# Layer 1 of a two-layer attention and expert kernel: the shared units of its feed-forward part moved behind the attention's drain, its experts' weights sent in another order and at other times

## The chip, the cores and the metric

The kernel runs on one core of one Trainium2 chip. A core has a matrix engine (TensorE, "PE", with its weight load "PEld"), a vector engine (VectorE, "DVE"), a scalar engine (ScalarE, "ACT"), a general engine (GpSimd, "POOL") that also issues the indexed DMAs, and a queue engine (SyncE, "SP") that issues the plain ones. They share an on-chip memory (SBUF), an accumulator memory (PSUM) of 8 banks, and 16 DMA engines to the main memory. The metric is the device time of one execution in microseconds; lower is better.

## The reference, cut to what matters

Eight sequences of 256 tokens, 256 wide, go through two layers, each an attention and a mixture of experts, each added to what came in. The part that is changed is the second mixture of experts:

```python
x = x + _L1_attn_ref(_layernorm(x), ...)
x = x + _L1_ffn_ref(_layernorm(x), ...)

def _moe_forward(...):                       # E = 32 experts, K = 8 chosen for each token
    scores = sigmoid(x @ router_w)           # 4 of 8 groups of experts, then the best 8
    routed = sum over the 8 chosen of gate * ((silu(x @ w_gate[e]) * (x @ w_up[e])) @ w_down[e])
    shared = (silu(x @ sw_gate) * (x @ sw_up)) @ sw_down      # for every token
    return routed + shared
```

All is computed in float32; the attention's projections are split in a high and a low part.

## The kernel before, in words

**Stages.** Attention 0, the mixture of experts 0, then one stage for layer 1: `attention(..., 1, ...)`, `finish`, `expert_blocks`. Within the stage each engine has one program, in the order in which these three functions emit it; engines meet by semaphores alone.

**Attention 1** is a software pipeline written out by hand. The outer loop runs over rounds `i` from -3 to B + 3 = 11 (B = 8 sequences), the inner over 8 steps `j`. In round `i` sequence `i` has its scores and maxima made, `i - 1` its exponentials and its product with the values, `i - 2` its output projection, and `i - 3` and `i - 4` the front of the mixture of experts. Rounds 9, 10 and 11 are the drain: no scores are left, only the last links of sequences 5 to 7.

**The front of one sequence m** is a chain over four engines: DVE adds the projection (`out_add`) and takes the statistics (`front_stats`), POOL makes the reciprocal deviation (`front_rstd`, step 1 of round m + 3), ACT applies it (`front_apply`), PE transposes (`front_transpose`, L698), ACT copies (`front_xT`, L904), PE makes the logits (`front_logits`, L707), ACT the exponential (`front_exp`, L911), DVE chooses (`route_groups` to `route_chosen`, L1136 to L1177), PE transposes the choice (`front_chosen`, L716), ACT copies (`front_chT`, L917), PE counts ranks (`front_ranks`, L726 to L733), DVE turns them into places (`route_places`, L1195 to L1206). That last instruction counts up `f_placed`.

**Scatters.** The token rows go to their experts' regions in main memory by 128 indexed DMAs of POOL (`scatter_rows`, L1553), 16 for each sequence, in order; those of sequence m wait for `f_placed` of m + 1. From round 4, step 3 on POOL issues two a step, so 74 are issued when round 8 ends, 90 after round 9; the last 6 are left to `finish`.

**Weights.** `wres` holds the 32 experts' weights of layer 1 (384 KB each) at the top of the SBUF. Experts 26 to 31 lie in free room and are loaded at the start of the stage. The others lie over attention 1's tiles. SP sends 25 down to 5 once all exponentials' inputs and maxima are done (`st_ps`, `max_done`), one for each count of the semaphore `paced`, which POOL counts up after every second scatter from number 78 on (`PACED`). Experts 0 to 4 go in one DMA in `finish`, once all sequences are placed.

**Shared units.** The shared expert is 8 units of 512 tokens and half the hidden width: `up` (PE, L1477, into banks 0 and 1 or 2 and 3), `silu` (ACT), `keep` (DVE, L1490), `down` (PE, L1496, into the same two banks), `add` (DVE, L1503). `up` of unit u waits for `add` of u - 2. Four units stand in the drain, at the steps that `unit_pe`, `unit_act` and `unit_dve` list (rounds 9 and 10), the other four in `finish`, between the links that make the table of blocks: `count` (L1850), `first` (L1855), `table` (L1860).

**Expert blocks.** 159 blocks of 128 rows, each loaded (`e_xg`, L1974), turned, multiplied and scattered back. SP loads the first rows when the table stands and all 128 scatters have landed. PE's first `up` (L1996) waits for all weights and for the eighth unit's `add`.

## Time and profile before

| | us |
|---|---|
| median of 3 runs | 1170.13 (1168.87 to 1175.76) |
| the profiled execution | 1172.08 |
| its span, from the first to the last instruction | 1169.5 |
| PE busy in the span | 899.2 (77%) |
| DVE, ACT, POOL busy | 685.6, 467.1, 621.2 |

The profile is one execution. Its page gives busy times, the chain of work that ended last, and the groups of instructions; the trace behind it answers for any stretch, engine or line. Times in its rows count from the start of the span. Mixture of experts 0 ends at about 475 us, attention 1 with its drain at about 800, `finish` at about 830, the expert blocks at about 1112; the rest sums up and stores.

### The profile page before, as it was taken

The page shows a single profiled execution, that of the slowest core. Times are in us where ns is not written, and L with a number is a line of the kernel's source. Part 1 is how long each engine was busy: PE and PEld are TensorE (multiplying, and loading weights), DVE is VectorE, ACT ScalarE, POOL GpSimd, SP SyncE. Part 2 cuts the span into 40 slices and gives each one's busy share as a digit, 9 for nine tenths or more (in the row PEclk, how much of TensorE's full clock was granted, in tenths as well). Part 3 has the DMA queues.
Part 4 walks back from the last instruction along what each step waited for, and adds up shares of the span by engine and source line. Part 5 has one row for each costly group of instructions (what it writes and reads, how often), then busy time and mean ns, then how long its engine had stood idle before and what let it go on. Part 6 is the DMA issues. An engine that isn't in the chain of part 4 may idle for free.

```text
span 1169.5 us, 22075 instructions
## 1 busy us (share of the span) xinstructions
PE 899.2 (77%) x5927; PEld 691.8 (59%) x5927; DVE 685.6 (59%) x2692; ACT 467.1 (40%) x1176; POOL 621.2 (53%) x870
## 2 busy tenths in 40 slices
PE   1687989878597992379987888856899999989900
PEld 1465667657355881256665565533688887778700
DVE  4678888865532554467687674352455544444568
ACT  2346666743112441257655443311344444444400
POOL 3646666523163652336558888755356655545500
PEclk9859999988798996559989576787999999999955
DMA  8500000000624543400002222566455655545287
GB/s 231 192 2 1 2 2 1 1 2 1 263 106 127 152 130 120 144 1 2 2 29 86 85 97 101 210 222 221 147 163 174 182 157 161 153 141 156 70 327 319
DMA packets 73093, 136.97 MB, mean 117 GB/s; under 512 B 13406, under 2 KB 51725, under 8 KB 70928
## 3 DMA queue, kind: packets, MB, share of 16 engines
q1 hardware_dynamic: 52144, 85.15, 22.8%
q0 software_dynamic: 17632, 46.73, 11.2%
q10 hardware_dynamic: 3200, 3.70, 0.9%
q8 instruction: 53, 0.87, 0.3%
q14 instruction: 64, 0.52, 0.2%
HBM read 79.15 MB, written 62.39 MB: 121 GB/s over the span
## 4 chain that ended last, share of the span: by engine, by line
PE 36%; DVE 9%; POOL 6%; issue 5%; ACT 2%; another core or an unknown queue 1%; DMA 1%; DVEq 0%; POOLq 0%; ACTq 0%; SPq 0%
PE s_psum L1996 12%; PE s_psum L2009 6%; PE s_psum L1988 3%; POOL rows L1553 3%; PE s_psum L1477 3%; PE s_psum L2004 2%; DVE a_masked L1074 2%; DVE f_rows L2096 2%; DVE f_xT L2096 2%; PE s_psum L549 1%; POOL a_probs L1414 1%; PE s_psum L1496 1%; PE s_psum L646 1%; PE s_psum L602 1%
## 5 line engine op out<-in xcount | busy, mean ns | idle before, releaser
L2106 POOL DMA_INDIRECT parts<-e_y,e_dest x206 | 202.7, 984 | 180.7 <-DVE e_y L2079 96.9
L1996 PE MATMUL s_psum<-wres,e_xT 128*128 x824 | 213.9, 382 | 1.8 <-ACT e_xT L2036 1.0
L1996 PEld LDWEIGHTS s_psum<-wres,e_xT 128*128 128x128 f32 x824 | 156.1, 191 | 26.1 <-issue 5.4
L1414 POOL TENSOR_SCALAR_AFFINE_SELECT a_probs<-a_probs 128x256 f32<-128x256 f32 x256 | 107.5, 444 | 117.6 <-ACT a_probs L870 116.8
L1553 POOL DMA_INDIRECT rows<-f_rows,f_place_at x128 | 125.2, 978 | 40.3 <-issue 31.7
L2009 PE MATMUL s_psum<-wres,e_hT 128*128 x412 | 125.3, 386 | 12.2 <-ACT e_hT L2046 11.6
L870 ACT ACTIVATE a_probs<-s_psum 128x768 f32<-128x768 f32 x128 | 104.6, 817 | 72.8 <-PE s_psum L629 68.2
L2041 ACT ACTIVATE e_act_out<-s_psum 128x128 f32<-128x128 f32 x206 | 57.1, 277 | 180.8 <-PE s_psum L1996 101.6
L2070 DVE TENSOR_TENSOR e_hid<-e_act_out,s_psum 128x128 f32<-128x128 f32 x206 | 59.0, 286 | 91.8 <-issue 42.6
L1074 DVE CUSTOM_DVE_ANT_0 a_masked<-s_psum,a_ahead 128x128 f32<-128x128 f32 (+1 forms) x256 | 76.1, 353 | 42.0 <-PE s_psum L605 39.1
L2079 DVE TENSOR_SCALAR e_y<-s_psum,e_xg 128x256 f32<-128x256 f32 x206 | 99.6, 484 | 0.7 <-issue 0.7
L2036 ACT ACTIVATE e_xT<-s_psum 128x256 f32<-128x256 f32 x206 | 79.0, 383 | 36.5 <-PE s_psum L1988 34.3
L1074 DVE CUSTOM_DVE_ANT_0 m_rows<-s_psum,a_ahead 128x128 f32<-128x128 f32 (+1 forms) x256 | 76.0, 352 | 23.4 <-PE s_psum L605 22.9
L2078 DVE COPY e_dest<-e_xg 128x1 int32 x206 | 31.7, 154 | 89.6 <-PE s_psum L2009 61.0
L1988 PE MATMUL s_psum<-ident,e_xg 128*128 128x128 f32 x412 | 79.5, 276 | 1.8 <-DMA e_xg<-rows 1.7
L1988 PEld LDWEIGHTS s_psum<-ident,e_xg 128*128 128x128 f32 x412 | 58.5, 142 | 23.7 <-issue 3.0
L2009 PEld LDWEIGHTS s_psum<-wres,e_hT 128*128 128x128 f32 x412 | 62.1, 191 | 16.4 <-issue 15.5
L549 PE MATMUL s_psum<-qkv_hi,a_yT_hi 128*128 128x512 f32 (+2 forms) x96 | 43.5, 453 | 29.5 <-DVE a_yT_lo L1003 20.9
L855 ACT ACTIVATE a_qT<-s_psum 128x512 fp32r<-128x512 f32 x64 | 38.3, 601 | 66.3 <-PE s_psum L582 66.3
L602 PE MATMUL s_psum<-a_kT,a_qT 64*128 64x128 f32 x256 | 46.4, 357 | 21.1 <-DVE a_neg_max L1074 19.5
L2004 PE MATMUL s_psum<-ident,e_hid 128*128 128x128 f32 x206 | 57.0, 277 | 3.5 <-issue 2.9
L2046 ACT ACTIVATE e_hT<-s_psum 128x128 f32<-128x128 f32 x206 | 56.8, 276 | 6.2 <-PE s_psum L2004 5.0
(297 smaller groups left out, 1993.4 us busy)
## 6 DMA issues: line engine op xcount, KB each, us to landing
e_xg<-rows SPq DMA_DIRECT2D x159, 160.0 KB
f_rows<-parts SPq DMA_DIRECT2D x8, 1024.0 KB, 7.2
f_xT<-parts SPq DMA_DIRECT2D x8, 1024.0 KB, 7.4
wres<-in_experts SPq DMA_DIRECT2D x21, 384.0 KB
e_xg<-rows SPq DMA_DIRECT2D x47, 144.0 KB
wres<-in_experts SPq DMA_DIRECT2D x4, 1536.0 KB
rows<-empty SPq DMA_DIRECT2D x1, 5120.0 KB, 24.1
e_yk<-parts SPq DMA_DIRECT2D x16, 256.0 KB, 2.9
```

Source lines behind the costliest of these rows:

```text
L870: nc.scalar.activation(probs[:, j % NPB], ring[:, 2:4, 0:TRI], ACT.Exp, scale=exp_scale).then_inc(exp_done, 1)
L1074: last = nc.vector.tensor_tensor_reduce(out=masked[:, j % 2, hh, cols], in0=ring[:, hh, cols], in1=ahead[:, cols], scale=-1.0, scalar=BIG, ...
L1414: last = nc.gpsimd.affine_select(out=diagonal[:, :, a], in_=diagonal[:, :, a], compare_op=ALU.is_ge, fill=0.0, base=0, pattern=[[0, 2], [1 ...
L1553: nc.gpsimd.indirect_dma_start(out=front["table"][:, :], out_offset=bass.IndirectOffsetOnAxis(ap=front["place_at"][:, t, k:k + 1], axis=0) ...
L1988: last = nc.tensor.transpose(ps_x[b % 2][:, c * P:(c + 1) * P], xg[b % NX][:, c * P:(c + 1) * P], ident[:])
L1996: last = nc.tensor.matmul(ps_u[b % 2][:, 0:2 * P], xT[b % 2][:, c * P:(c + 1) * P], wres[:, ds(e, 1), 2 * c * P:2 * (c + 1) * P].rearrange ...
L2004: nc.tensor.transpose(ps_h[b % 2][:, 0:P], hid[b % 2][:], ident[:]).then_inc(h_ps, 1)
L2009: nc.tensor.matmul(ps_y[b % 2][:, 0:H], hT[b % 2][:], wres[:, ds(e, 1), D:D + H].rearrange("p a n -> p (a n)"), start=True, stop=True).the ...
L2036: nc.scalar.activation(xT[b % 2][:], ps_x[b % 2][:, 0:H], ACT.Copy).then_inc(xT_done, 1)
L2070: nc.vector.tensor_tensor(hid[b % 2][:], act_out[b % 2][:], ps_u[b % 2][:, P:2 * P], ALU.mult).then_inc(hid_done, 1)
L2079: nc.vector.tensor_scalar(y[b % NY][:], ps_y[b % 2][:, 0:H], pair[:, ds(e, 1), 0], None, ALU.mult).then_inc(y_done, 1)
L2106: nc.gpsimd.indirect_dma_start(out=parts[:, :], out_offset=bass.IndirectOffsetOnAxis(ap=dest[b % NY][:], axis=0), in_=y[b % NY][:], in_off ...
```

## The change

Four edits, all in layer 1:

- The tables `unit_pe`, `unit_act` and `unit_dve` are gone. All 8 units are in `finish`, behind all of the attention on each engine. On PE `up` of 0 and 1 come ahead of `count`; `first` comes behind `up` 2, `table` behind `up` 3.
- Weights: all of 25 down to 0 are single DMAs of SP in attention 1, each for one count of `paced`. 25 to 19 wait for the last transposes of the stacked tile (`group_ps`), 18 to 16, 15 to 13 and 12 to 5 for the shifted scores of ever later sequences, 4 to 0 for the last places. For this the tiles are allocated in another order.
- `paced` is counted up once a step in the 13 steps from round 7, step 0, and from round 9 on after every fourth scatter.
- Scatters: two a step up to round 9, one a step in rounds 10 and 11. So 106 are issued in the attention and 22 in `finish`.

```diff
-FREE_EXPERTS, LAST_EXPERTS = 26, 5
-PACED = 78
+STACK_EXPERTS, FIRST_QUERY_EXPERTS, SECOND_QUERY_EXPERTS = 19, 16, 13
+ROUND_STEPS = 13
+PACE = 4
...
-    unit_pe, unit_act, unit_dve = {}, {}, {}
-    if front is not None:
-        unit_pe = {(B + 1, 0): [("up", 0)], (B + 1, 2): [("up", 1)], (B + 1, 3): [("down", 0)], (B + 1, 5): [("down", 1)],
-                   (B + 1, 7): [("up", 2)], (B + 2, 1): [("up", 3)], (B + 2, 2): [("down", 2)], (B + 2, 6): [("down", 3)]}
...
-                sp.wait_ge(st_ps, PAIRS * B)
-                sp.wait_ge(max_done, PAIRS * B)
-                for n, e in enumerate(range(FREE_EXPERTS - 1, LAST_EXPERTS - 1, -1)):
+                sp.wait_ge(group_ps, NF * B)
+                for n, e in enumerate(range(FREE_EXPERTS - 1, -1, -1)):
+                    if e == STACK_EXPERTS - 1:
+                        sp.wait_ge(st_ps, PAIRS * (B - 2))
+                    if e == FIRST_QUERY_EXPERTS - 1:
+                        sp.wait_ge(st_ps, PAIRS * (B - 1))
+                    if e == SECOND_QUERY_EXPERTS - 1:
+                        sp.wait_ge(st_ps, PAIRS * B)
+                        sp.wait_ge(max_done, PAIRS * B)
+                    if e == LAST_EXPERTS - 1:
+                        sp.wait_ge(f_placed, B)
                     sp.wait_ge(front["paced"], n + 1)
                     sp.dma_start(env["wres"][:, e], front["w_experts"][e]).then_inc(front["wres_loaded"], 16)
...
                     if front is not None and (i, j) >= (4, 3):
-                        for _ in range(2):
+                        for _ in range(2 if i <= B + 1 else 1):
                             m = scattered // (TB * TOPK[layer])
                             if scattered % (TB * TOPK[layer]) == 0:
                                 pool.wait_ge(f_placed, m + 1)
                             scatter_rows(nc, front, layer, scattered)
-                            if scattered >= PACED and scattered % 2:
+                            scattered += 1
+                            if i > B and scattered % PACE == 0:
                                 passed(pool, front["paced"])
-                            scattered += 1
+                        if (B - 1, 0) <= (i, j) < (B - 1 + ROUND_STEPS // PAIRS, ROUND_STEPS % PAIRS):
+                            passed(pool, front["paced"])
...
-                if n % 2:
+                if n % PACE == PACE - 1:
                     passed(pool, front["paced"])
...
+            units["up"](pe, 0)
+            units["up"](pe, 1)
             count()
-            units["up"](pe, begun)
-            first()
-            units["up"](pe, begun + 1)
-            for u in range(begun, NU):
+            for u in range(end):
                 units["down"](pe, u)
-                if u == begun:
+                if u + 2 < end:
+                    units["up"](pe, u + 2)
+                if u == 0:
+                    first()
+                if u == 1:
                     table()
-                if u + 2 < NU:
-                    units["up"](pe, u + 2)
```

## Rows read from the trace of the kernel before

**Rows 1.** Stretches of attention 1 and drain: us, then each engine's busy us, PEclk, DMA share, GB/s
```profile
700.00:731.00 31.00, 26.85 (x181) 18.66 (x181) 13.83 (x66) 11.08 (x18) 26.23 (x42) 0.68 0.28 102
...
740.00:750.00 10.00, 8.54 (x51) 5.47 (x50) 4.23 (x12) 2.77 (x5) 7.62 (x10) 1.00 0.76 243
...
780.00:790.00 10.00, 0.39 (x2) 0.15 (x2) 4.79 (x27) 0.00 (x0) 7.56 (x9) 0.65 0.89 357
790.00:800.00 10.00, 1.57 (x6) 1.42 (x6) 0.66 (x5) 1.66 (x2) 4.77 (x5) 0.50 0.27 98
```

**Rows 2.** Units in rounds 9 and 10: busy us of L1477, then of L1496
```profile
731.00:761.00 30.00, 9.25 (x16) 3.71 (x16) 0.76 0.59 208
...
731.00:761.00 30.00, 5.65 (x16) 4.01 (x16) 0.76 0.59 208
```

**Rows 3.** Timeline of POOL: start, us, what, idle before and its releaser
```profile
758.54 0.96 POOL L1553 DMA_INDIRECT rows<-f_rows,f_place_at  x1 [0.30 <-issue]
759.80 0.96 POOL L1553 DMA_INDIRECT rows<-f_rows,f_place_at  x1 [0.30 <-issue]
769.11 0.23 POOL L1348 TENSOR_SCALAR a_f_var_eps<-a_f_mv 128x2 f32<-128x2 f32 x1 [8.35 <-DVE a_f_mv L1131]
...
770.47 0.22 POOL L1354 TENSOR_TENSOR a_f_shift<-a_f_neg_mean,a_f_rstd 128x2 f32<-128x2 f32 x1
...
821.79 0.96 POOL L1553 DMA_INDIRECT rows<-f_rows,f_place_at  x1 [0.30 <-issue]
```

**Rows 4.** Timelines of the front of sequence 7, and of one link of sequence 6
```profile
752.90 1.92 PE L707 MATMUL s_psum<-router,f_xT 128*128 128x32 f32 x8 [4.26 <-issue]
...
758.63 0.22 ACT L911 ACTIVATE a_f_exp<-s_psum 128x64 f32<-128x64 f32 x1 [4.48 <-DMA e_yk<-parts]
...
770.73 1.09 ACT L898 ACTIVATE f_rows<-x,a_f_shift,a_f_rstd 128x256 f32<-128x256 f32 x2 [2.87 <-POOL a_f_shift L1354]
...
775.75 0.60 PE L698 MATMUL s_psum<-ident,f_rows 128*128 128x128 f32 x4
...
776.38 0.60 ACT L904 ACTIVATE f_xT<-s_psum 128x512 f32<-128x512 f32 x1 [3.63 <-issue]
...
777.03 1.08 PE L707 MATMUL s_psum<-router,f_xT 128*128 128x32 f32 x8 [0.69 <-issue]
...
778.55 0.24 DVE L1136 TENSOR_SCALAR a_scores<-a_f_exp 128x64 f32<-128x64 f32 x1 [1.38 <-issue]
...
784.41 0.22 DVE L1177 TENSOR_TENSOR a_chosen_r<-a_replaced,a_eligible 128x64 fp32r<-128x64 f32 x1 [1.54 <-remote]
...
784.69 0.39 PE L716 MATMUL s_psum<-ident_r,a_chosen_r 128*32 128x128 f32 x2 [4.78 <-issue]
...
790.80 0.37 ACT L917 ACTIVATE a_chT<-s_psum 32x256 fp32r<-32x256 f32 x1 [12.29 <-remote]
...
791.23 0.42 PE L726 MATMUL s_psum<-a_base_r,ones_r 128*128 128x64 f32 x1 [6.14 <-issue]
...
792.19 0.60 PE L733 MATMUL s_psum<-tri_r,a_chT 32*128 32x32 f32 x2
...
799.30 0.19 DVE L1195 TENSOR_TENSOR f_cum<-f_cum,a_chosen_both 128x32 fp32r<-128x32 f32 x1 [9.86 <-remote]
```

**Rows 5.** Timelines of `finish` and of the first block
```profile
800.42 5.16 PE L1477 MATMUL s_psum<-f_xT,f_ws 128*128 128x512 f32 x8
...
811.01 0.80 PE L1860 MATMUL s_psum<-d_lists,d_ones 32*128 32x318 f32 x2
...
826.48 3.02 PE L1496 MATMUL s_psum<-f_ws,u_hid 128*128 128x256 f32 x8 [1.91 <-DVE u_hid L1490]
...
831.40 1.12 PE L1996 MATMUL s_psum<-wres,e_xT 128*128 x4 [1.05 <-ACT e_xT L2036]
...
811.12 1.23 DVE L1503 TENSOR_TENSOR x<-s_psum,x 128x1024 f32<-128x1024 f32 x1 [2.70 <-issue]
...
817.86 1.22 DVE L1503 TENSOR_TENSOR x<-s_psum,x 128x1024 f32<-128x1024 f32 x1 [4.54 <-PE s_psum L1496]
```

**Rows 6.** Timeline of SP's queue
```profile
770.48 10.73 SPq L1322 DMA_DIRECT2D wres<-in_experts  x10
...
825.41 24.47 SPq L1974 DMA_DIRECT2D e_xg<-rows  x20
```

More of the change, by code:

```diff
@@ L391, in attention, with query_homes @@
             place_top = sb("place_top", [P, TB, 8])
+        pieces = NH // 2 + (NK // 2 if multi else 1)
+        def query_homes(i):
+            return (sb(f"qT{i}", [P, PAIRS, N], F32R), sb(f"kT{i}", [P, PAIRS if multi else 1, N], F32R))
+        ahead = sb("ahead", [P, TRI])
+        masked = wide("masked", [P, 2, 2, TRI])
+        max_stack = sb("max_stack", [P, TB, 2, 2 * NH, 2], F32R)
+        maxT = sb("maxT", [P, TRI], F32R)
+        pairs_by_age = {i: query_homes(i) for i in (1, 0, 2)}
+        qT, kT = ([pairs_by_age[i][n] for i in range(NQ)] for n in range(2))
         yT_hi = sb("yT_hi", [P, FC, N], F32R)
@@ L402, in attention @@
         rotated = wide("rotated", [P, TB, QK])
-        pieces = NH // 2 + (NK // 2 if multi else 1)
         stack = sb("stack", [P, TB, pieces * P], F32R)
-        qT = [sb(f"qT{i}", [P, PAIRS, N], F32R) for i in range(NQ)]
-        kT = [sb(f"kT{i}", [P, PAIRS if multi else 1, N], F32R) for i in range(NQ)]
-        ahead = sb("ahead", [P, TRI])
-        masked = wide("masked", [P, 2, 2, TRI])
-        max_stack = sb("max_stack", [P, TB, 2, 2 * NH, 2], F32R)
-        maxT = sb("maxT", [P, TRI], F32R)
         m_E = EXPERTS[0]
@@ L808, in _ @@
                             moe_logits(int(name[1]))
-                    for name, u in unit_pe.get((i, j), []):
-                        if u == 0 and name == "up":
-                            pe.wait_ge(shared_loaded, 16)
-                            pe.wait_ge(exp_done, PAIRS * B)
-                            pe.wait_ge(max_done, PAIRS * B)
-                        front["units"][name](pe, u)
         @block.scalar
@@ L977, in _ @@
                         ln_apply(i + 3)
-                    if (i, j) in unit_act:
-                        front["units"]["silu"](act, unit_act[i, j])
         @block.vector
@@ L1299, in _ @@
                         moe_apply(m)
-                    for name, u in unit_dve.get((i, j), []):
-                        front["units"][name](dve, u)
             dve.wait_ge(out_added, B)
@@ L1798, in finish @@
     make_sem, psum, block = shared_stage
-    placed, wres_loaded, units, begun = front["placed"], front["wres_loaded"], front["units"], front["units_begun"]
+    placed, units, end = front["placed"], front["units"], NU
     with ExitStack() as ctx:
@@ L1861, in table @@
                                  skip_group_check=True).then_inc(tab_ps, 1)
+            pe.wait_ge(front["shared_loaded"], 16)
+            pe.wait_ge(front["exp_done"], PAIRS * B)
+            pe.wait_ge(front["max_done"], PAIRS * B)
+            units["up"](pe, 0)
+            units["up"](pe, 1)
             count()
[L1864 to L1867 removed]
+            for u in range(end):
                 units["down"](pe, u)
[L1869 removed]
+                if u + 2 < end:
[3 more added lines that the diff above has]
+                if u == 1:
                     table()
[L1871 to L1872 removed]
         @block.scalar
         def _(act):
[L1876 removed]
+            for u in range(end):
                 units["silu"](act, u)
@@ L1887, in _ @@
             dve.wait_ge(ones_made, 1)
+            units["keep"](dve, 0)
             dve.wait_ge(count_ps, 1)
@@ L1892, in _ @@
             nc.vector.tensor_copy(blocks[:], blocks_i[:]).then_inc(blocks_done, 1)
-            units["keep"](dve, begun)
+            units["add"](dve, 0)
+            units["keep"](dve, 1)
             dve.wait_ge(blocks_done, 1)
@@ L1903, in _ @@
             nc.vector.tensor_tensor(lists[:, NB:2 * NB], owned[:], start[:], ALU.mult).then_inc(lists_done, 1)
-            units["add"](dve, begun)
+            units["add"](dve, 1)
+            units["keep"](dve, 2)
             dve.wait_ge(tab_ps, 1)
             nc.vector.tensor_copy(tab[0:1, 0:2 * NB], ps_r[0:1, 0:2 * NB]).then_inc(tab_done, 1)
-            for u in range(begun + 1, NU):
+            units["add"](dve, 2)
+            for u in range(3, end):
                 units["keep"](dve, u)
```

15 lines of the change are left out of this document (3 added, 12 removed).

## The prediction

> **What bounds the kernel now.** I read the views in this order: the page's slices and its chain of waits, the busy times by stretch, then the timelines of each engine between the end of round 8 (about 734 us) and the first expert block.
>
> The change touches nothing outside layer 1's attention, drain and `finish`. In rounds 7 and 8 POOL is busy 26.23 of 31 us; what is left are its short gaps between instructions, and the chain of waits of that stretch runs over POOL's scatters and cuts [rows 1]. So the dense rounds are paced by POOL, and the DMA engines are used at 28% there. In the drain no engine is full. The front of a sequence is a chain of single instructions over four engines, and PE has four units woven in: 9.25 + 5.65 = 14.9 us of them before 761 us [rows 2], all in PE's order ahead of links that the chain waits for. In `finish` PE sets the pace: a unit every 817.86 - 811.12 = 6.74 us, and the first block's product starts at 831.40, right behind the eighth unit [rows 5]. The weights and the rows are not what ends last there: SP sends the first row loads at 825.41 [rows 6], four microseconds before PE is free.
>
> What stands out is time in which nobody works. From 785 to 799 us PE is nearly idle at the lower clock (granted 0.5 in 790:800, that is 1.2 GHz) [rows 1], and the consumers start late behind work that has ended: ACT's exponential of sequence 6 at 758.63, where the logits ended at 752.90 + 1.92 = 754.82, 3.8 us late; ACT's copy at 790.80, where PE's transposes ended at 784.69 + 0.39 = 785.08, 5.7 us late; DVE's first place at 799.30, where the ranks ended at 792.19 + 0.60 = 792.79, 6.5 us late; DVE's choice itself 1.5 us late [rows 4]. The profile names "remote" or nothing as releaser. I call these late handovers. They fall in stretches in which POOL issues scatters without pause and, just before, SP's weights fill the DMA engines (76 and 89% [rows 1]). The sum below depends on whether they stay.
>
> **The change, part by part.**
>
> *Dense rounds.* 13 weight loads of 384 KB are added, one in each of 13 steps; scatters per step stay two. POOL's additional instruction is a semaphore count, which before cost nothing visible: the gap in front of a scatter is the same 0.30 us at 758.54 and 821.79 whether a count stood there or not [rows 3]. The DMA engines have room: 28% used, and a load a step is less dense than 740:750, where they ran at 76% while POOL's scatters kept their 7.62 us of 10 [rows 1]. I take 0; its bounds are 0 and 3 us, by the thought that two or three handovers in these 13 steps come late by one more microsecond.
>
> *Drain, sequence 6 and the first part of 7.* The 14.9 us of units leave PE's order here. The statistics of sequence 7, which came at 769.11 and left POOL idle for 8.35 us [rows 3], come earlier by about that and by the 3.8 us handover if it is mended: near 752. But POOL then isn't ready. Its scatters of round 9 run on, one every 1.26 us, and the one at 758.54 (the single one of round 10, step 0) ends at 759.50 [rows 3]. So `front_rstd` of sequence 7 starts at 759.8 in place of 769.11: a gain of 9.3 us, not 17. It also means that lateness of up to 7 us ahead of this point costs nothing. It takes 770.47 + 0.22 - 769.11 = 1.6 us, to 761.4.
>
> *Drain, the rest of 7.* From rows 4: apply 1.09, transposes 0.60 at the full clock (I take 1.1, as the logits took 1.08 and 1.92 at the two levels), copy 0.60, logits 1.92, from there to DVE's first instruction 778.55 - 778.11 = 0.44, choice 784.41 + 0.22 - 778.55 - 1.54 = 4.54, transposes 0.39, copy 0.37, ranks 792.79 - 791.23 = 1.56. Sum 12.0, with half a microsecond for the handovers between them 12.5. The ranks end at 761.4 + 12.5 = 773.9, the places a microsecond later. Before, the ranks ended at 792.79.
>
> For PE's pieces I take the prices at 1.2 GHz, since with the units gone nothing fills PE in the drain, and in 790:800, where it did only such pieces, the granted clock was 0.50 [rows 1]. At 2.4 GHz the sum is 2.0 us less (0.5 + 0.84 + about 0.7), and the first unit would start warm, 5.16 - 3.7 = 1.5 less; that is the lower bound, -3.5. The Trainium skill (TensorE: Matmul & The Clock Gate, "What's actually happening") says that an idle PE is clocked at half rate; by it alone the slow prices hold, and the trace agrees with its 0.50. It speaks against moving work out of the drain.
>
> *Finish.* PE now starts unit 0 right behind the ranks, without waiting for the places, at 773.9. Four units took from 800.42 to 826.48 + 3.02 = 829.50, 29.1 us, slow start and slow last `down` included [rows 5]. Four more at 6.74 us are 27.0. `table` stood in the pause ahead of `up`, and now stands behind it: 0.8 us [rows 5]. DVE's list of blocks stands ahead of `add` 1 and delays `up` 3 by about 0.6. Together 57.5: the last `down` ends at 831.4 in place of 829.50, 1.9 us later.
>
> *Behind it.* POOL: from 761.4 on 37 scatters (91 to 127) at 1.26 us end at about 808, against 821.79 + 0.96 before [rows 3]; even with waits for landings they stay ahead of 829. Weights: the last follows scatter 123, at about 803, and is there by 810. Both are hidden behind the units by some 20 us; if that cover were gone they would count. SP's new waits for weights stand ahead of the row loads only, which need the table and all scatters anyway. POOL's sequencer counts `paced` when it reads past the scatters, not when they run: SP sent ten loads in 770.48 to 781.21, while the twenty scatters that pace them took twice as long [rows 6]. So "every fourth scatter" will be bursts of about four, not a stream. The Trainium skill (Advanced Engine Details and Errata, "Sequencer Loop") says that a sequencer reads and queues further instructions while earlier ones execute; the trace agrees, with these ten loads in 10.73 us.
>
> *The late handovers.* On the chain of sequence 7 they cost 1.5 + 5.7 + 6.5 = 13.7 us before. If the weights' traffic is the cause they mostly go, since bursts are now four loads and not ten. If POOL's unbroken scatters or PE's idleness are the cause they stay, because both remain, and PE idles more. So they cost between 0 and 13.7; I take 5. For the shorter bursts speaks that links at 767 to 769 us, with no traffic, were prompt; for the other that the last one at 799.30 came when the DMA share was 27% [rows 1].
>
> Sum: +1.9 + 5 = +6.9 us. The profiled execution took 1172.08, 2.6 more than its span 1169.5, and stands 1.95 over the median of 1170.13. I carry the difference to the median: 1177.0.
>
> **The rivals.**
>
> 1. *Handovers stay half late* (the forecast): +3 to +11 us, 1173 to 1181. Chance 0.41.
> 2. *Handovers become prompt.* Only the weights made them late. +1.9, and down to -1.6 at the full clock: 1168.5 to 1172.5. For it: late ones cluster behind bursts of 7 and 10 loads. Against it: bursts of four remain, and 799.30. Chance 0.27.
> 3. *Slower: the handovers stay as late as before.* The place is the front of sequence 7, from 761 to 775 us, price the whole 13.7: +15.6, 1185.7. It decides from 9.8 us of lateness on, where +1.9 + 9.8 reaches 1%. For it: POOL scatters without pause through all of it, and lateness before was worst with PE idle. Chance 0.24.
> 4. *Weights slow the dense rounds.* If each of 13 steps waits 1.2 us longer for something the loads hold up, 15.6 us, 1187 to 1193. Against it: 740:750, where POOL kept its pace. Chance 0.05.
> 5. *Faster by over 1%.* It needs 11.7 us. The drain can end no earlier than POOL lets it, and 8 units behind it take at least 54; that gives -1.6. Only if the lateness also sits in something that I don't see, such as the last scatters' landing, is there more. Chance 0.03.
>
> **How the numbers follow.** The forecast is rival 1's middle, 1177.0. Its own range is 1173 to 1181. The range that should hold 8 in 10 takes in rival 2's and most of rival 3: 1167 to 1189. One per cent (11.7 us) is about what a measurement of this kernel can tell from no change. Faster by over 1%: 0.03. Slower: rivals 3 and 4, 0.29, of which 0.01 stays under the bound, 0.28. Within 1%: 0.69.
>
> **What would show it.** Right: in the drain no `u_` tile; POOL's L1348 of sequence 7 at about 759.8 with no idle time before it; L716 to L733 of sequence 7 done near 774 plus the lateness; then 8 periods of 6.74 us on PE without a break up to 831 plus the lateness; the first e_xg load long before the last `down`; the expert blocks as before. The number that decides is the time from POOL's L1354 to PE's last L733, 12.5 us if handovers are prompt, up to 26 if not. Wrong: rounds 7 and 8 longer than 31 us for the same steps, POOL's sequence-7 statistics waiting for DVE again, or PE waiting in front of its first L1996 for weights.

## The result, and the profile after

The changed kernel took 1182.8 us (median of five runs, 1176.3 to 1192.4) beside 1169.4 us (1166.3 to 1175.8) for the kernel before: the ratio is 1.0147, with a 95% interval of 1.0098 to 1.0197. So it is slower, by 13.5 us. The forecast of 1177.0 is 5.8 us too low, and the time lies inside the range of 1167 to 1189. Throughout, an execution over 1.5% above the fastest of its kernel in the same session is left out of medians and ratios; that touched two of the kernel before and one of run 4. The profiled execution is the slowest of the five, 1192.38 us with a span of 1189.9, 20.4 us over the span of before; so the split below is that of a slow execution, and no trace splits the 13.5 us of the medians. These are the lines of it that answer to those of before, in the order of the chain. First POOL's and ACT's timelines (start, us, what, idle time before it and its releaser).

```profile
766.00 0.23 POOL L1343 TENSOR_SCALAR a_f_var_eps<-a_f_mv 128x2 f32<-128x2 f32 x1
...
767.30 0.20 POOL L1349 TENSOR_TENSOR a_f_shift<-a_f_neg_mean,a_f_rstd 128x2 f32<-128x2 f32 x1
```

```profile
774.70 0.22 ACT L901 ACTIVATE a_f_exp<-s_psum 128x64 f32<-128x64 f32 x1 [4.28 <-issue]
...
797.88 0.60 ACT L1481 ACTIVATE u_act_out<-s_psum 128x512 f32<-128x512 f32 x1 [11.90 <-DMA rope_gamma<-in_k_gamma]
```

DVE's timeline: the last instruction of the choice, three of the places, and the first `keep`.

```profile
782.45 0.23 DVE L1165 TENSOR_TENSOR a_chosen_r<-a_replaced,a_eligible 128x64 fp32r<-128x64 f32 x1 [3.09 <-remote]
...
788.83 0.19 DVE L1183 TENSOR_TENSOR f_cum<-f_cum,a_chosen_both 128x32 fp32r<-128x32 f32 x1 [1.82 <-remote]
...
792.95 0.29 DVE L1192 MAX8 a_place_top<-a_place 128x8 f32<-128x32 f32 x2 [3.66 <-remote]
795.06 0.17 DVE L1194 CAST f_place_at<-a_place_top 128x16 int32<-128x16 f32 x1 [1.82 <-remote]
...
799.43 0.69 DVE L1487 TENSOR_TENSOR u_hid<-s_psum,u_act_out 128x512 f32<-128x512 f32 x1 [3.94 <-DMA setup_tri<-in_tri]
```

PE's timeline from the logits of sequence 7 to the first block (L1474 is `up`, L1493 `down`), and SP's queue.

```profile
770.48 1.91 PE L703 MATMUL s_psum<-router,f_xT 128*128 128x32 f32 x8 [0.69 <-ACT f_xT L894]
783.87 0.40 PE L712 MATMUL s_psum<-ident_r,a_chosen_r 128*32 128x128 f32 x2 [11.48 <-DVE a_chosen_r L1165]
...
785.70 0.60 PE L729 MATMUL s_psum<-tri_r,a_chT 32*128 32x32 f32 x2
786.24 9.36 PE L1474 MATMUL s_psum<-f_xT,f_ws 128*128 128x512 f32 x16
...
800.18 3.03 PE L1493 MATMUL s_psum<-f_ws,u_hid 128*128 128x256 f32 x8 [3.51 <-DVE u_hid L1487]
804.53 5.31 PE L1474 MATMUL s_psum<-f_xT,f_ws 128*128 128x512 f32 x8 [1.32 <-DVE x L1500]
...
850.74 2.42 PE L1493 MATMUL s_psum<-f_ws,u_hid 128*128 128x256 f32 x8 [1.92 <-DVE u_hid L1487]
...
855.06 2.07 PE L1994 MATMUL s_psum<-wres,e_xT 128*128 x4 [1.05 <-ACT e_xT L2034]
```

```profile
685.84 125.53 SPq L1316 DMA_DIRECT2D wres<-in_experts  x26
822.53 46.62 SPq L1972 DMA_DIRECT2D e_xg<-rows  x16
```

The reader is to see four things. POOL comes to the reciprocal deviation of sequence 7 without idle time, at 766.00 (before 769.11, after 8.35 us of waiting [rows 3]). Between the links there is still time in which nobody works: ACT's exponential starts at 774.70 though the logits ended at 770.48 + 1.91 = 772.39, and DVE's own successive instructions, which need nothing but each other, come 3.09, 3.66 and 1.82 us apart. The first `down` stands at 800.18, 4.6 us behind the end of both `up`, because its `keep` on DVE waits behind those late places and behind ACT's late `silu`. And the rows and weights are no part of it: SP sends the first row loads at 822.53, 30 us before PE is free for them.

The trace behind these rows also holds the times at which semaphores counted, though not of every count. It shows where a late handover is lost: not between the count and the consumer, but between the producer's end and the count (us).

| kernel | producer, its end | its count | consumer, its start |
|---|---|---|---|
| before | PE, logits of 6: 754.81 | 758.61 | ACT, exponential: 758.63 |
| before | PE, ranks of 7: 792.80 | 799.21 | DVE, first place: 799.30 |
| changed | DVE, replaced values: 779.37 | 782.43 | DVE, choice: 782.45 |
| changed | DVE, product for the places: 789.29 | 792.93 | DVE, maxima: 792.95 |
| run 2 | PE, logits of 7: 772.50 | 785.43 | ACT, exponential: 785.45 |
| run 5 | PE, `down`: 800.08 | 819.11 | DVE, `add`: 819.13 |
| run 7 | PE, `down`: 815.59 | 848.45 | DVE, `add`: 848.47 |

The consumer stands ready and starts 0.02 to 0.09 us behind the count, so its instructions were not late. (Runs 2, 5 and 7 are experiments below.)

This is how the 20.4 us between the two profiled executions divide, split at the last pair of cuts of round 8 (733.27 and 739.66), the last rank and the first block's product:

| stretch | before | after | difference | forecast |
|---|---|---|---|---|
| up to the last cuts | 733.3 | 739.7 | +6.4 | 0 |
| to the end of the last rank | 59.5 | 46.6 | -12.9 | -18.9, or -13.9 with 5 us of lateness |
| to the first block's product | 38.6 | 68.8 | +30.2 | +20.8 |
| to the end | 338.1 | 334.8 | -3.3 | 0 |

### The profile page after: what moved, and what is told of

Read it like the earlier page. It is cut to its first block, busy times and chain, and to the rows that moved or that the text cites. A ratio compares the mean times of both kernels' runs of the same rounds, so it can differ in the third digit from the quotient of the medians.

```text
span 1189.9 us, 22097 instructions
## 1 busy us (share of the span) xinstructions
PE 919.0 (77%) x5927; PEld 707.2 (59%) x5927; DVE 688.3 (58%) x2692; ACT 461.7 (39%) x1172; POOL 621.5 (52%) x870
## 4 chain that ended last, share of the span: by engine, by line
PE 37%; DVE 9%; POOL 6%; issue 5%; ACT 2%; another core or an unknown queue 2%; DMA 1%; DVEq 0%; POOLq 0%; ACTq 0%; SPq 0%
PE s_psum L1994 11%; PE s_psum L2007 6%; POOL rows L1550 3%; PE s_psum L1986 3%; PE s_psum L1474 2%; PE s_psum L545 2%; DVE f_rows L2094 2%; DVE f_xT L2094 2%; PE s_psum L2002 1%; DVE a_masked L1062 1%; PE s_psum L1493 1%; POOL a_probs L1409 1%; PE s_psum L598 1%; PE s_psum L642 1%
## 5 line engine op out<-in xcount | busy, mean ns | idle before, releaser
L2034 ACT ACTIVATE e_xT<-s_psum 128x256 f32<-128x256 f32 x206 | 79.2, 384 | 32.0 <-PE s_psum L1986 27.3
L625 PE MATMUL s_psum<-a_maxT,sel_head 64*128 64x384 f32 x256 | 58.2, 452 | 0.0
```

The costliest lines, as they stand in the source:

```text
L2034: nc.scalar.activation(xT[b % 2][:], ps_x[b % 2][:, 0:H], ACT.Copy).then_inc(xT_done, 1)
```

## The experiments

The runs were made in four sessions on three chips, the last two sessions on the same chip: runs 1 to 4, then 5 to 7 and the changed kernel again, then 8 and 9, then 10 and 11. The medians of the kernel before in them were 1172.2, 1171.5, 1163.8 and 1135.4 us, so each time is compared only with the kernel before of its own session. (Part of that is the stretch behind the first block: 338.1 us in the first profile of before, 319.4 and 319.7 in runs 10 and 11.) What is compared across sessions are distances within a trace: from the shift of sequence 7 to its last rank, and from there to the end of the last `down` (all in us). The start of the first block counts from the start of the span. Lateness is what a chain or a unit takes over its prompt length. Each row is one profiled execution; the ratio is from all executions. Run 7 was executed once, and its additional scatters make its total meaningless.

| kernel | shift of 7 to last rank | last rank to last `down` | first block | ratio to before |
|---|---|---|---|---|
| before | 22.1 | 36.7 (4 units) | 831.4 | 1 |
| changed | 18.8 | 66.9 | 855.1 | 1.0147 |
| changed, once more | 24.0 | 64.6 | 860.6 | 1.0273 (1.0184 to 1.0361) |
| 1 weights alone | 17.9 | 50.1 (4 units) | 838.6 | 1.0103 (1.0053 to 1.0153) |
| 2 units alone | 32.1 | 58.4 | 856.9 | 1.0262 (1.0172 to 1.0353) |
| 3 no weights in the drain | 23.3 | 58.2 | 846.2 | 1.0129 (1.0034 to 1.0224) |
| 4 none in rounds 10 and 11 | 19.0 | 72.9 | 867.2 | 1.0244 (1.0140 to 1.0348) |
| 5 scatters held | 12.2 | 86.9 | 870.5 | 1.0301 (1.0214 to 1.0387) |
| 6 held early | 12.2 | 87.3 | 862.3 | 1.0251 (1.0171 to 1.0331) |
| 7 short rows | 25.0 | 104.3 | 892.5 | - |
| 8 small instruction between | 21.6 | 66.8 | 850.8 | 1.0190 (1.0137 to 1.0244) |
| 9 rest behind each fourth | 12.2 | 56.6 | 855.7 | 1.0160 (1.0111 to 1.0210) |
| 10 early, rest behind each eighth | 12.2 | 58.2 | 831.8 | 1.0143 (1.0100 to 1.0185) |
| 11 before, four rests | 11.3 | 30.9 (4 units) | 819.2 | 1.0105 (1.0070 to 1.0139) |

### First question: which part of the change costs, the weights or the units?

**1. Weights alone.** The changed kernel with the unit tables of before and `finish` of before.

```diff
+    unit_pe, unit_act, unit_dve = {}, {}, {}      # and the tables and loops of the kernel before
...
-            units["up"](pe, 0)
-            units["up"](pe, 1)
             count()
+            units["up"](pe, begun)
+            first()
```

> The changed kernel with its units back at their old places in the drain (rounds 9 and 10, four of them) and the old order of the second half; the weights and the scatters stay as changed. Theory W (13 loads in rounds 7 and 8 slow the dense rounds by 6 to 9 us, as the trace of the changed kernel shows 36.4 + 30.5 us for two rounds that took 32.1 + 25.8): 1176 to 1179, and the two rounds stay over 65 us. Theory U (the 13.5 us come from the units' new place alone, and the longer rounds are the clock of one execution): 1168 to 1172, and the two rounds are back at 58 to 60 us. Half of each, my own guess: about +7.

**2. Units alone.** The kernel before, with the tables taken out and `finish` of the changed kernel (the same diff the other way).

> The kernel before with one thing changed: all eight units stand behind the drain, in the changed kernel's order; weights (21 in one chain from the end of round 8 on, 5 at the end) and scatters as before. Theory W: the units cost about 6 us (1174 to 1177), and rounds 7 and 8 take 58 us as before. Theory U: 1180 to 1184. Rival: the long chain of single loads in the drain makes the handovers of sequence 7 as late as before (13.7 us), then 1184.

Run 1 came out 1.0% slower and run 2 2.6% slower. The changed kernel, which has both, had been 1.5% slower in the first comparison and was 2.7% slower when it was run again. With such a spread the ratios can't tell how the parts add up; the traces have to. Theory W was wrong about the cost of the loads. In run 1 a stretch of 31 us in the two rounds with the loads moved twice the bytes of before (208 GB/s in place of 97) with POOL as busy (26.22 us in both):

```profile
682.00:713.00 31.00, 27.51 (x227) 19.21 (x225) 22.61 (x126) 13.15 (x21) 26.22 (x42) 0.72 0.67 208
```

The distance from the last cuts of round 6 to the last cuts of round 8 is 54.4 us before (678.83 to 733.27) and 54.5 to 54.8 in runs 1 to 11, nine of which have the 13 loads. The loads cost nothing there. Only the changed kernel itself needs 58.3, in both of its profiles. POOL's timeline of the changed kernel, then of run 3, which differs from it by one wait of SP that lies far behind:

```profile
681.33 0.76 POOL L1409 TENSOR_SCALAR_AFFINE_SELECT a_probs<-a_probs 128x256 f32<-128x256 f32 x2 [3.61 <-ACT a_probs L860]
...
712.44 0.76 POOL L1409 TENSOR_SCALAR_AFFINE_SELECT a_probs<-a_probs 128x256 f32<-128x256 f32 x2 [3.60 <-ACT a_probs L860]
...
739.66 0.78 POOL L1409 TENSOR_SCALAR_AFFINE_SELECT a_probs<-a_probs 128x256 f32<-128x256 f32 x2
```

```profile
680.36 0.78 POOL L1410 TENSOR_SCALAR_AFFINE_SELECT a_probs<-a_probs 128x256 f32<-128x256 f32 x2
...
734.95 0.76 POOL L1410 TENSOR_SCALAR_AFFINE_SELECT a_probs<-a_probs 128x256 f32<-128x256 f32 x2 [0.15 <-ACT a_probs L860]
```

The loss is two waits of POOL, a round apart, at 681.33 and 712.44 (in its second profile at 683.99, 3.21 us, and 715.10, 3.74 us). Between 620 us and the last cuts no other trace has a wait of POOL of over 1 us. Each time POOL waits for ACT's exponentials and ACT for PE, and PE is busy without pause at the granted clock 0.50, that is 1.2 GHz. These are windows of the changed kernel up to the first and up to the second wait, then of run 3 in the same step as the second:

```profile
670.00:676.00 6.00, 6.00 (x29) 5.16 (x30) 3.70 (x17) 1.69 (x4) 5.03 (x9) 0.50 0.30 111
676.00:682.00 6.00, 6.00 (x43) 4.01 (x42) 3.05 (x20) 1.41 (x2) 2.09 (x4) 0.54 0.15 55
...
700.00:706.00 6.00, 6.00 (x41) 4.77 (x34) 2.26 (x13) 1.92 (x4) 5.06 (x8) 0.50 0.76 231
706.00:712.00 6.00, 6.00 (x32) 4.40 (x36) 3.12 (x19) 0.54 (x1) 2.37 (x4) 0.50 0.43 147
```

```profile
702.00:708.00 6.00, 3.73 (x41) 2.40 (x41) 5.44 (x37) 1.71 (x3) 5.12 (x8) 1.00 0.75 249
```

So two steps that PE did at half rate make the 6.4 us up to the last cuts; each lengthened its round by 3.7 to 3.8 us, and the changed kernel had been 1.1 us ahead before them. The first of them lies ahead of the first weight load at 685.84, and the clock stood at 0.53 in 646:682, where run 3 had 0.75 with the same program; the loads can't be the cause of that one. Why the clock was low in this kernel alone stays open.

In run 2 most of the loss sits in one handover. The logits of sequence 7 end at 772.50, ACT's exponential starts at 785.45, 12.95 us later, and ACT does nothing in between:

```profile
785.45 0.22 ACT L895 ACTIVATE a_f_exp<-s_psum 128x64 f32<-128x64 f32 x1 [14.91 <-DMA e_yk<-parts]
```

The releaser named there, a transfer of the stage before, had long been done. So the question became what makes handovers late. None of the three expectations for run 2 (1174 to 1184) comes near the 1200.5 measured.

### Second question: what makes handovers late?

**3. No weights in the drain.**

```diff
                     if e == SECOND_QUERY_EXPERTS - 1:
                         sp.wait_ge(st_ps, PAIRS * B)
                         sp.wait_ge(max_done, PAIRS * B)
+                        sp.wait_ge(f_placed, B)
```

> The changed kernel, but experts 12 to 0 all wait for the last places, so that no weight load lies in rounds 9 and 10, where the front of sequence 7 runs; the scatters stay. Theory L (weights' traffic makes the handovers late): the time from the shift of sequence 7 to its last rank falls from 18.8 us to 12.5 to 14, the end comes 5 us earlier, 1178. Theory S (POOL's unbroken scatters make them late): it stays at 18 to 20 us, 1183. The last weights land at about 825 us of the span, still ahead of the first block.

The chain got longer, 23.3 us, though no weight load lay beside it. Theory L falls: the weights' traffic isn't needed (SP sends none between 721.97 and 794.06). PE's timeline of this run, logits and the transposes of the choice, 15.89 us apart where 4.9 are enough:

```profile
765.80 1.92 PE L703 MATMUL s_psum<-router,f_xT 128*128 128x32 f32 x8 [0.74 <-issue]
783.61 0.40 PE L712 MATMUL s_psum<-ident_r,a_chosen_r 128*32 128x128 f32 x2 [15.89 <-DVE a_chosen_r L1165]
```

**4. No scatters in rounds 10 and 11.**

```diff
-                        for _ in range(2 if i <= B + 1 else 1):
+                        for _ in range(2 if i <= B + 1 else 0):
```

> The changed kernel, but rounds 10 and 11 issue no scatters, so that 38 are left for the part behind the drain; POOL is empty while the front of sequence 7 runs from its shift on. Theory S: the time from the shift of sequence 7 to its last rank falls from 18.8 us to 12.5 to 14. Theory L: it stays, apart from what four weight loads fewer take away (16 to 19). In both the last scatters come some 18 us later, at about 832 to 838, and the last weight soon behind scatter 124; that is about when the first block is ready, so the time may win nothing: 1178 to 1184.

This one was badly made. POOL's program goes on into `finish`, where the next scatter needs only the places of its own sequence, so the row of scatters went on at once, in the same stretch. The 19.0 us say nothing on the theories.

**5. Scatters held** from the shift of sequence 7 until all places stand.

```diff
-                        for _ in range(2 if i <= B + 1 else 1):
+                        for _ in range(2 if i <= B + 1 else 1 if (i, j) <= (B + 2, 0) else 0):
...
-                pool.wait_ge(placed, n // (TB * K) + 1)
+                pool.wait_ge(placed, B)
```

> The changed kernel with one thing changed: POOL issues no scatter from the shift of sequence 7 until all places stand (91 issued before, 37 after). The run in which rounds 10 and 11 issued none did not do this, since the part behind the drain began its scatters at once. Theory S (POOL's unbroken row of scatters makes the handovers late): from the shift of sequence 7 to its last rank 12.5 to 14 us in place of 18.8, places within 2 us of it, first block's product about 61 us after the last rank; 1172 to 1177. Theory L (weights' traffic does it): no more than 4 us won in the chain. Theory I (it is PE's or the engines' idleness): nothing won, and the scatters end later, 1185 to 1190.

**6. Held early.** As 5, but from round 9, step 6 on, and `if n % 2:` for the count in `finish`.

> As the run that holds the scatters, but they already stop after step 5 of round 9 (86 issued, 42 left), so that POOL is free for the reciprocal deviation of sequence 7 as soon as DVE has its statistics; behind the drain a load of weights follows every second scatter. Theory S: last rank about 768 us of the span, the first block's product at 826 to 830 (before: 831.4), so 1166 to 1171. Theory I: as the changed kernel or slower, 1182 to 1190.

Here is the clearest pair of readings of the study. With POOL quiet, the chain from the shift to the last rank takes 12.2 us in both runs, at a granted clock of 0.50, and every handover is prompt. So the sum of its links in the prediction (12.5) was right, and PE's idleness (theory I) is no cause. But both totals missed what theory S expected, 1172 to 1177 and 1166 to 1171: they came to 1211.5 and 1202.0. For then POOL has 37 or 42 scatters to do in one unbroken row beside the units, and the lateness moves there. PE's and DVE's timelines of run 5:

```profile
794.31 3.70 PE L1474 MATMUL s_psum<-f_xT,f_ws 128*128 128x512 f32 x8 [1.32 <-DVE x L1500]
...
798.09 1.99 PE L1493 MATMUL s_psum<-f_ws,u_hid 128*128 128x256 f32 x8
820.41 5.48 PE L1474 MATMUL s_psum<-f_xT,f_ws 128*128 128x512 f32 x8 [20.34 <-DVE x L1500]
```

```profile
819.13 1.23 DVE L1500 TENSOR_TENSOR x<-s_psum,x 128x1024 f32<-128x1024 f32 x1 [16.08 <-remote]
```

PE's `down` ended at 800.08; DVE's `add`, free since 803.05, started at 819.13. One handover cost 16 us, and the kernel became 3.0% slower. About a dozen scatters had gone out since 783.07 before the first late handover, and once the row had ended (last scatter at 829.70) one more count came late, at 835.29, and then the units fell into their 6.74 us. It is not a matter of the profiled execution alone: the four executions of run 5 took 1203 to 1214 us, the seven of the kernel before beside them 1165 to 1182.

**7. Short rows.** Scatters 74 to 105 carry 64 of 320 values, to a table of their own; the real ones follow behind the places.

```diff
-        out=front["table"][:, :],
+        out=front["table"][:, :] if n < 74 or whole else front["short"][:, :],
...
-        in_=front["rows"][:, t], in_offset=None)
+        in_=front["rows"][:, t] if n < 74 or whole else front["rows"][:, t, 0:64], in_offset=None)
```

> The changed kernel, in which scatters 74 to 105 carry 64 of a row's 320 values to a table that nobody reads, and the real 74 to 127 all follow behind the last places; so a fifth of the bytes and the same number of scatters and descriptors in the drain. The whole time is some 40 us longer and says nothing; only the front of sequence 7 is read. If the bytes of the scatters make the handovers late: 12.5 to 15 us from the shift to the last rank. If POOL's instructions or their descriptors do: 18 us or more.

The chain took 25.0 us with a fifth of the bytes, and during the long row behind it one unit waited 34 us. So the lateness doesn't come from the bytes of the scatters.

```profile
783.84 0.39 PE L712 MATMUL s_psum<-ident_r,a_chosen_r 128*32 128x128 f32 x2 [16.10 <-DVE a_chosen_r L1165]
...
849.75 5.42 PE L1474 MATMUL s_psum<-f_xT,f_ws 128*128 128x512 f32 x8 [34.16 <-issue]
```

**The changed kernel again.**

> The changed kernel once more, on the chip and beside the runs of the variants. Its first profile showed two rounds with weight loads at 36.4 + 30.5 us where three variants, two of them with the same loads, had about 58 together. If the loads cost time in the dense rounds it shows 65 us again, if that was one execution's slow clock 58 to 60. Total 1179 to 1186.

58.3 us for the two rounds again, from cuts to cuts, as in the first profile (the 36.4 + 30.5 us of the expectation were counted otherwise). So it is not the clock of one execution alone, and not the cost of the loads, as said. The chain took 24.0 us, and the whole was 2.7% slower than the kernel before beside it, against 1.5% in the first comparison. The size of the lateness is not a constant of the kernel.

**8. A small instruction between** the scatters, **9. a rest behind each fourth.**

```diff
     nc.gpsimd.indirect_dma_start(...)
+    if n >= 74:                                        # run 8
+        nc.gpsimd.memset(front["spacer"][:, n - 74:n - 73], 0.0)
...
+    if n >= 74 and n % IN_FLIGHT == IN_FLIGHT - 1:     # run 9
+        for landed in front["scattered"]:
+            nc.gpsimd.wait_ge(landed, 16 * (n // IN_FLIGHT + 1))
```

> The changed kernel, with one small instruction of POOL (a constant into 128x1) behind each scatter from number 74 on, so that the row of scatters is no longer unbroken but POOL is as busy as before; 54 times about 0.2 to 0.4 us more for POOL. Theory R (what matters is that scatters follow each other with nothing between them): the stalls of up to 20 us behind the drain go, the last rank comes 12.5 to 14 us behind the shift of sequence 7, and the kernel takes 1172 to 1178. Theory B (what matters is that POOL never rests or how many scatters it issues in a time): stalls as before, 1190 to 1205 on this chip's kind.

> The changed kernel, in which POOL waits behind every fourth scatter from number 74 on until all have landed, so that it rests for about 2 us in every 7. Theory B: the stalls go, as in the run before; the last scatter comes some 25 us later (about 840 us), so the sum wins less, 1178 to 1190. Theory R: also mostly gone, since each rest breaks the row; the two together tell whether a busy break is enough. If neither run loses its stalls, scatters aren't the cause at all, though the run that held them back had a prompt chain.

Run 8 kept its lateness (21.6 us in the chain, a stall of 7.65 in the units). Its small instruction took 0.11 us inside the gap that was there anyway, and the scatters still came every 1.27 us. Run 9 lost it altogether. POOL's, then PE's timeline of run 9:

```profile
782.49 0.97 POOL L1550 DMA_INDIRECT rows<-f_rows,f_place_at  x1 [2.46 <-DMA rows<-f_rows,f_place_at]
```

```profile
790.40 0.60 PE L729 MATMUL s_psum<-tri_r,a_chT 32*128 32x32 f32 x2
...
818.04 3.70 PE L1474 MATMUL s_psum<-f_xT,f_ws 128*128 128x512 f32 x8 [1.32 <-DVE x L1500]
...
824.78 3.70 PE L1474 MATMUL s_psum<-f_xT,f_ws 128*128 128x512 f32 x8 [1.32 <-DVE x L1500]
...
854.20 0.66 PE L1989 MATMUL s_psum<-ident,e_xg 128*128 128x128 f32 x2 [6.59 <-DMA e_xg<-rows]
```

Chain 12.2 us, eight units in 56.6, no stall, all links prompt, while POOL issues just as many scatters beside them. Its last rank is late only because POOL, resting, comes to `front_rstd` of sequence 7 at 777.31; and now the scatters end last, so PE waits 6.59 us for rows. That POOL's scatters, issued one behind the other for tens of microseconds, make the other engines' handovers late is thus shown from both sides: hold them or let POOL rest (5, 6, 9) and the lateness is gone where they are held, change the bytes, the weights or what stands between them (3, 7, 8) and it stays. Whether the rest matters or the lower rate (four scatters in 7.2 us in place of 5.1) is open, and so is the mechanism. The number of scatters that have not yet landed is no good candidate: in `finish` POOL waits for the landing of scatter n - 4 before it issues n, and run 5's row, all of it in `finish`, was late nevertheless. Two readings look like something that fills up and drains, which is argued and not shown: from a pause on it took 10 scatters (before, from 770.86) or about 12 (run 5, from 783.07) until the first late count, but only 4 in the changed kernel, whose row had been broken for just the 1.7 us of `front_rstd`; and counts still came late some 5 us behind the end of run 5's row. The Trainium skill (SBUF — State Buffer, "Who interferes with whom") says that DVE and GpSimd can lock each other out of a port that they share, and that PE and ACT never wait on anyone. That doesn't cover these readings: in run 2 it is ACT that starts 12.95 us late on PE's result, and POOL keeps its 0.96 us through all of it.

### Third question: what is the change worth with prompt handovers?

**10. Early and rests behind each eighth**, a version meant to beat both; **11. the kernel before with four rests.**

```diff
-PACE = 4                                                  # run 10
+PACE = 3
-                        for _ in range(2 if i <= B + 1 else 1):
+                        for _ in range(2 if (i, j) < (B + 1, 6) else 0 if (i, j) < (B + 2, 1) else 1):
...
+    if n >= 74 and n % 8 == 7:                            # run 11: and n < 111
+        for landed in front["scattered"]:
+            nc.gpsimd.wait_ge(landed, 16 * (n // IN_FLIGHT + 1))
```

> A version that could beat both: the changed kernel, with POOL waiting for all landings behind every eighth scatter from number 79 on, no scatters from round 9, step 6 until the shift of sequence 7 (so that this comes at about 757 us), and a weight load for every third scatter. If rests of about 2.3 us each 10 us are enough against the stalls: last rank at 769 to 771, then eight units of 6.74 us without a break, last scatter at about 822, first block's product at 828 to 832 (before: 831.4), total 0 to 5 us faster than the kernel before. If eight scatters in a row are already too many: stalls of 5 to 20 us, and 5 to 25 us slower than before.

> The kernel before, with the same wait for all landings behind scatters 79, 87, 95 and 103 alone; all else as it was. The two in round 9 fall into POOL's idle 8.35 us before the statistics of sequence 7, the two behind cost it 4.6 us, most of it time in which it waits for the last places anyway. If unbroken scatters cause the late handovers of before too: last rank at 782 to 786 in place of 792.8, places within 2 us, but the first block hangs on the last scatter (about 824 us), so 2 us faster to 2 us slower. If they have another cause in this kernel: last rank at 790 or later, and 2 to 6 us slower.

Neither trace has a late handover of over 1 us. PE's timeline of run 10: last rank, eight units in 58.2 us, the first block 1.9 us behind the last `down`. PE is the bound.

```profile
771.10 0.60 PE L729 MATMUL s_psum<-tri_r,a_chT 32*128 32x32 f32 x2
...
827.47 2.43 PE L1493 MATMUL s_psum<-f_ws,u_hid 128*128 128x256 f32 x8 [1.92 <-DVE u_hid L1487]
831.80 2.07 PE L1997 MATMUL s_psum<-wres,e_xT 128*128 x4 [0.33 <-issue]
```

POOL's and PE's timelines of run 11, four units woven in the drain:

```profile
759.07 0.23 POOL L1348 TENSOR_SCALAR a_f_var_eps<-a_f_mv 128x2 f32<-128x2 f32 x1
...
811.98 0.96 POOL L1553 DMA_INDIRECT rows<-f_rows,f_place_at  x1 [0.30 <-issue]
```

```profile
771.48 0.39 PE L733 MATMUL s_psum<-tri_r,a_chT 32*128 32x32 f32 x2
...
800.77 1.99 PE L1496 MATMUL s_psum<-f_ws,u_hid 128*128 128x256 f32 x8 [1.91 <-DVE u_hid L1490]
817.86 1.46 PE L1991 MATMUL s_psum<-ident,e_xg 128*128 128x128 f32 x4 [15.10 <-DMA e_xg<-rows]
```

The last rank comes at 771.9, ten microseconds earlier than expected, POOL has no idle time in front of `front_rstd`, and PE has finished all units at 802.8 and then waits 15.10 us for the rows of the last scatters. The first block comes at 819.2, 12.6 us ahead of run 10. This pair is the nearest thing to the change with prompt handovers, but not a clean one: run 10 also holds its scatters for three steps, rests more often and sends its weights at other times. And the two profiles lie further apart than the kernels: run 11's is the fastest of its six executions (1140.7), while the medians, 1153.4 and 1147.1, differ by 6.2 us. So the change costs something like 6 us with prompt handovers by the medians, 13 by the profiles; that it wins nothing is what the pair shows.

Against the kernel before of that session neither won: 1.4% and 1.0% slower. The kernel before has no profile there. From the block part of runs 10 and 11 (319.4 and 319.7 us from the first block to the end) I estimate its first block at 1135.4 - 2.3 - 319.6 = 813.5. Run 11's median of 1147.1 gives by the same sum 1147.1 - 1.8 - 319.6 = 825.7, some 12 us later. If so, the kernel before had almost no lateness left to mend in that session, and the rests, which only delay the last scatter, cost what they took; this is an estimate, no trace shows it. I found no version that beats the kernel before.

## Why the prediction came out as it did

The time lies inside the range, and slower is the way that was forecast, but the size is about half: +6.9 us forecast, +13.5 measured. By its own classes the prediction gave 0.69 to "within 1%" and 0.28 to "slower"; the ratio of 1.0147, with its interval's lower end at 1.0098, is the latter. Rival 3 (+15.6 us) came nearest.

- **POOL bounds the start of sequence 7's last part: right.** `front_rstd` stood at 766.00 with no idle time before it. It was forecast for 759.8; the 6.2 us between are the later last cuts.
- **The gain of 9.3 us up to there: the number right, the cause wrong.** From the last cuts to `front_rstd` the kernel before took 35.8 us and the changed one 26.3, a gain of 9.5. I ascribed POOL's 8.35 us of waiting [rows 3] to the 14.9 us of units ahead of the links [rows 2]. The trace of before has two late handovers on that path. One is the exponential of sequence 6, 3.8 us late [rows 4], which I saw; behind it DVE, free since 761.17, starts an `add` only at 763.71, though PE's `down` had ended at 754.63 + 3.76 = 758.39. These are 6.3 of the 8.35 us:

```profile
754.63 3.76 PE L1496 MATMUL s_psum<-f_ws,u_hid 128*128 128x256 f32 x8
...
763.71 1.22 DVE L1503 TENSOR_TENSOR x<-s_psum,x 128x1024 f32<-128x1024 f32 x1 [2.55 <-issue]
```

  Runs 11 and 10, with the units in the drain and without, show the path with prompt handovers. The statistics of sequence 7 end 24.3 us behind the last cuts (727.17) in run 11, and 18.8 us behind them (735.83) in run 10. The units cost 5.5 us there, but POOL, with 19 or 20 scatters to issue first, isn't ready before 26.3 (changed kernel) or 27.6 (run 2), so they cost the chain nothing:

```profile
751.21 0.25 DVE L1131 BATCH_NORM_AGGREGATE a_f_mv<-a_f_stats 128x2 f32<-128x6 f32 x2
```

```profile
754.36 0.25 DVE L1119 BATCH_NORM_AGGREGATE a_f_mv<-a_f_stats 128x2 f32<-128x6 f32 x2
```

  From the last cuts to the last rank run 11 took 44.7 us and run 10 35.9. POOL's six scatters more (7.6 us), its one rest more (2.2) and a chain that is 0.9 us shorter account for the 8.8 us between them. What the units in the drain give is 58.2 - 30.9 = 27.3 us of PE's work that need not follow. The forecast paid 27 us for it and booked against it a chain that was shorter by 18.9 us, of which the part that came from late handovers was not the units' to give back.
- **The chain of 12.5 us: right** where handovers are prompt (12.2 in four runs). In the changed kernel it took 18.8, 6.3 of it lateness. The deciding number thus lay half way between the two readings that the prediction set, 12.5 and 26.
- **57.5 us for eight units: right when prompt** (56.6 and 58.2), too short here: 66.9. The 5 us for lateness were put on the chain alone, while it went on for as long as POOL scattered: late places (795.06), late `silu` (797.88), and `keep` 0 behind both in DVE's order. Lateness was 6.3 + 9.4 = 15.7 us in all, where the forecast had 5. Rival 3, which gave 13.7 to the front of sequence 7, was near in size, but over half of it lay in `finish`.
- **Weights and scatters hidden by some 20 us: right**, and by more. The last weight left at 811.4, the first rows at 822.5, PE came for them at 853.
- **Dense rounds at 0 (0 to 3): right for the loads**, by nine runs; rival 4 falls. But the changed kernel lost 6.4 us up to the last cuts, in two steps that PE did at 1.2 GHz, the first of them ahead of any load. The sum had no term for that, and its cause is open.
- **The cause of the lateness: mis-judged.** Taking 5 of 13.7 us rested on the weights' bursts as a good part of the cause; runs 3, 5 and 9 say that it is the scatters. "Bursts are now four loads and not ten" was no reason for hope. That the links at 767 to 769 us were prompt has a likelier reason in the same rows: POOL had stood idle for 8.35 us. It is argued, not tested.

In the two profiles the misses add up: forecast 6.9, later cuts 6.4, lateness 15.7 - 5 = 10.7, and 3.3 less behind the first block (unexplained) make 20.7, against 20.4 measured. So the two terms that were too small, lateness and the dense rounds, lie on the same side. Measured against the profiled execution the forecast (1172.1 + 6.9 = 1179.0) missed by 13.4 us; that it stands 5.8 from the median, and inside the range, owes something to luck, and the range holds because rival 3 was given its room.

## What to carry to other kernels

A wait in a trace has two possible owners, the work ahead of it and a handover that came late; before a gain is booked for moving work away, look whether the same link was prompt elsewhere with the same work ahead of it. And compare kernels by their medians: one profile can be the fastest or the slowest of its kernel, as two were here. Where one engine issues indexed DMAs for tens of microseconds without rest, price every handover beside it as uncertain, and expect the lateness to follow the scatters when they are moved. And work that fills an engine's idle time in a drain is worth its whole length; taking it out pays only if the chain that it stood in gets shorter by more.

## What the runs showed of the hardware

- Beside an unbroken row of POOL's indexed DMAs (0.96 us each, one every 1.27) the semaphore counts of PE and DVE came up to 19.0 us behind the end of their instruction in run 5 (800.08 to 819.11) and 32.9 us in run 7 (815.59 to 848.45); the consumer started within 0.1 us of the count. ACT, PE and DVE itself were kept waiting by it. In run 5 the first dozen scatters of the row did no harm.
- Rests of 2.5 us behind every fourth or eighth scatter removed it; an instruction of 0.11 us between them didn't, nor did rows with a fifth of the bytes, nor taking the weight loads away.
- 13 loads of 384 KB in two dense rounds, with the DMA engines at 67% in place of 26%, cost no time that can be seen (54.5 to 54.8 us against 54.4).
- The same program of PE can get a different clock: from 646 to 682 us the granted clock was 0.53 and 0.51 in the two profiles of the changed kernel and 0.75 in run 3, with PE busy 32.2, 32.0 and 28.7 us.
- The median of the same kernel differed by 3.2% between sessions (1135.4 to 1172.2 us), and by 2.5% between two on the same chip (1135.4 and 1163.8), more than the change is worth; the changed kernel's ratio to before was 1.015 in one session and 1.027 in another.
